# A transformer block on one core: the bias table written from 128 partitions, its other traffic on a second queue, and the experts' gathers issued one pair ahead

## The reference

```python
x = x + attn(layernorm(x))              # 16 heads, additive bias by distance, causal, then a small MLP
x = x + xattn(layernorm(x), ctx, ctx)   # 8 heads, differential weights, then an MLP with two norms
x = x + ffn(layernorm(x))               # 8 experts, each token goes to the nearest centroid's expert

# in attn
bias = rel_bias[bucket]                          # (S, S, 16), bucket depends on key - query alone
attn = (einsum(q, k) + bias) * scale             # scale: one factor per head
attn = softmax(where(causal, attn, -1e6))
# in ffn, for the expert e of a token
h = xn @ up_w[e]; a, g = split(h)
out = (a * silu(g)) @ down_w[e] + skip
```

## Time and profile before

| | us |
|---|---|
| three runs: lowest, median, highest | 1495.56, 1496.47, 1498.79 |
| the profiled execution, whole | 1503.02 |
| its span, on which all rows lie | 1501.3 |
| first score product of stage A starts | 73.56 |
| first expert product starts | 1205.11 |

### The profile page before, as it was taken

One profiled execution on the slowest core, in us unless ns is written; L12 is line 12 of the kernel. 1 busy time (PEld: TensorE's weight loads), 2 busy tenths in 40 slices (PEclk: granted clock), 3 DMA queues, 4 the chain that ended last, 5 costly groups with the idle time before them and its releaser, 6 DMA issues.

```text
span 1501.3 us, 27047 instructions
## 1 busy us (share of the span) xinstructions
PE 1287.7 (86%) x8806; PEld 933.9 (62%) x8807; DVE 813.5 (54%) x2080; ACT 554.3 (37%) x1179; POOL 429.2 (29%) x657
## 2 busy tenths in 40 slices
PE   3187999999999999999999999999997288888887
PEld 1055767777676777767677776767775145555544
DVE  3245566765768667576767757686654611211111
ACT  1224353543535354363635445363531022121211
POOL 2110203231322324132232413223222333434342
PEclk9578999999999999999999999999999589999998
DMA  6910000000000000000000000000063011111111
GB/s 90 288 31 15 1 15 11 20 28 0 28 0 28 4 24 23 5 28 0 28 0 28 18 10 28 0 28 8 16 230 134 14 50 51 53 49 49 48 59 25
DMA packets 44483, 58.77 MB, mean 39 GB/s; under 512 B 6549, under 2 KB 38111, under 8 KB 44192
## 3 DMA queue, kind: packets, MB, share of 16 engines
q1 hardware_dynamic: 38832, 43.87, 10.1%
q0 software_dynamic: 5616, 14.43, 3.3%
HBM read 42.54 MB, written 16.66 MB: 39 GB/s over the span
## 4 chain that ended last, share of the span: by engine, by line
PE 54%; DVE 16%; issue 11%; POOL 7%; ACT 5%; DMA 5%; SPq 3%; POOLq 0%; DVEq 0%; ACTq 0%
PE bank L1302 49%; DMA shared<-rows_x,shared 4%; POOL shared L883 3%; ACT shared L700 2%; PE bank L1464 2%; DVE a_p L1121 2%; POOL out_rows L901 2%; ACT a_p L695 1%; DVE a_sq L1081 1%; SPq L552 1%; DVE shared L998 1%; PE bank L1323 1%; POOL shared L778 1%; DVE shared L953 1%; DVE shared L1090 1%
## 5 line engine op out<-in xcount | busy, mean ns | idle before, releaser
L1302 PE MATMUL bank<-shared 128*128 128x256 f32 (+4 forms) x2242 | 449.9, 381 | 35.3 <-POOL shared L878 11.3
L1302 PEld LDWEIGHTS bank<-shared 128*128 128x128 f32 (+2 forms) x2242 | 319.4, 174 | 115.9 <-issue 32.4
L1121 DVE TENSOR_TENSOR a_p<-a_p,eb 128x385 f32<-128x385 f32 x256 | 125.9, 555 | 75.7 <-ACT a_p L695 75.7
L1302 PE MATMUL bank<-up,shared 128*128 x312 | 139.6, 601 | 0.9 <-issue 0.9
L845 POOL TENSOR_SCALAR a_rz<-a_ms 128x2 f32<-128x2 f32 x16 | 3.1, 193 | 418.8 <-ACT a_sq L706 418.8
L695 ACT ACTIVATE a_p<-bank 128x385 f32<-128x385 f32 x256 | 105.2, 503 | 41.6 <-PE bank L1302 41.5
L1302 PE MATMUL bank<-a_xnT,w 128*128 128x256 f32 x512 | 114.7, 382 | 1.4 <-ACT a_xnT L612 1.4
L1302 PE MATMUL bank<-w,a_hT 128*128 128x256 f32 x512 | 113.1, 379 | 0.0
L1302 PEld LDWEIGHTS bank<-a_xnT,w 128*128 128x128 f32 x512 | 96.0, 190 | 18.0 <-issue 3.4
L1302 PEld LDWEIGHTS bank<-w,a_hT 128*128 128x128 f32 x512 | 97.3, 190 | 13.2
L961 DVE TENSOR_SCALAR shared<-shared 128x256 f32<-128x256 f32 x128 | 67.5, 578 | 68.3 <-POOL shared L778 62.2
(11 more groups left out here) (197 smaller groups left out, 2128.9 us busy)
## 6 DMA issues: line engine op xcount, KB each, us to landing
up<-in_L_ffn_up_w SPq DMA_DIRECT2D x8, 1024.0 KB, 13.8
x_in<-in_x SPq DMA_DIRECT2D x16, 256.0 KB, 2.7
shared<-in_ctx SPq DMA_DIRECT2D x16, 256.0 KB, 2.9
rows_x<-shared SPq DMA_DIRECT2D x16, 256.0 KB, 2.2
rows_skip<-shared SPq DMA_DIRECT2D x16, 256.0 KB, 2.3
down<-in_L_ffn_down_w SPq DMA_DIRECT2D x8, 512.0 KB, 12.3
toep<-a_hT SPq DMA_DIRECT2D x1, 3072.0 KB, 33.3
eb<-toep SPq DMA_DIRECT2D x2, 1024.0 KB, 7.4
```

What stands on the lines that cost most here:

```text
L1121: tt(a_p[:, n_ % NPA], a_p[:, n_ % NPA], eb[:, n_], ALU.mult).then_inc(sig["a_p"], 1)
L1302: return mm(out, lhsT=lhsT, rhs=rhs, start=first, stop=last, **kw)
```

## The change

**The bias.** The scale is multiplied into the 32 x 16 table ahead of the product, and the table is laid eight times side by side (`COPIES = 8`), so that the product gives every head's row on eight partitions, 128 in all. `toep` is written from these 128 partitions, each of which writes 16 of the 128 copies of its head. The loads that this needs go first on SP. The value and output weights, the write of the maxima and their read back are issued by ACT, on its own DMA queue, at the head of its program. Subtraction, exponential and mask work on four parts of four heads, and each group of scores waits for its own part. `w0v` is scaled ahead of the first turn, and the first batch's `A.v` stands where that of the other batches does.

**The experts.** `m_in` of pair k + 2 is gathered in step k, once the tiles of pair k + 1 have been transposed, and the gathers of pairs 0 and 1 are issued ahead of the first step. PE's order within a pair is new: the second tile's up product is split around the first tile's transpose, and the next pair's `transpose_in` stands ahead of the second tile's down product.

```diff
-    mrow = nc.dram_tensor("mrow", (H0, S), F32, kind="Internal")
+    mrow = nc.dram_tensor("mrow", (H0, COPIES, S), F32, kind="Internal")
...
-    bd = flat_h[0:H0, S:S + 3 * P]
-    bmax = flat_h[0:H0, S + 3 * P:2 * S + 3 * P]
+    bd = flat_h[:, S:S + 3 * P]
+    bmax = flat_h[:, S + 3 * P:2 * S + 3 * P]
+    relb_rows = flat_h[0:BUCKETS, 2 * S + 3 * P:2 * S + 4 * P].rearrange("b (h g) -> b h g", g=COPIES)
...
     def _(sp):
+        for dst, src in bias_loads:
+            sp.dma_start(dst, src).then_inc(s_bias, 16)
         sp.dma_start(x_in[:], of_batch(x_tiles, 0)).then_inc(sig["a_loaded"], 16)
...
         sp.wait_ge(s_bd, 2)
-        sp.dma_start(toep.ap(), bd.unsqueeze(1).to_broadcast([H0, P, 3 * P])).then_inc(s_toep, 16)
-        sp.wait_ge(s_bmax, 2)
-        for t in range(T):
-            sp.dma_start(mrow.ap()[:, tok(t)], bmax[:, tok(T - 1 - t)]).then_inc(s_toep, 16)
-        for dst, src in v_loads:
-            sp.dma_start(dst, src).then_inc(s_v, 16)
-        sp.wait_ge(s_toep, 48)
+        by_row = toep.ap().rearrange("h (g i) m -> (h g) i m", g=COPIES)
+        sp.dma_start(by_row, bd.unsqueeze(1).to_broadcast([P, P // COPIES, 3 * P])).then_inc(s_toep, 16)
+        sp.wait_ge(s_toep, 16)
...
     def _(act):
+        for dst, src in v_loads:
+            nc.scalar.dma_start(dst, src).then_inc(s_v, 16)
+        act.wait_ge(s_bmax, 2)
+        by_row = mrow.ap().rearrange("h g q -> (h g) q")
+        for t in range(T):
+            nc.scalar.dma_start(by_row[:, tok(t)], bmax[:, tok(T - 1 - t)]).then_inc(s_mrow, 16)
         act.wait_ge(s_setup_dma, ALL_LOADED)
         nc.scalar.activation(lam[:, 1:2], lam[:, 0:1], ACT.Exp, scale=-1.0).then_inc(s_lam, 1)
+        act.wait_ge(s_mrow, 16 * T)
+        maxima = mrow.ap()[:, 0].rearrange("(o h) q -> o h q", o=1)
+        for half, loaded in enumerate((s_tp1, s_tp2)):
+            nc.scalar.dma_start(bias_max[half], maxima[:, half * 8:(half + 1) * 8, :].to_broadcast([P, 8, S])
+                                ).then_inc(loaded, 16)
...
-        def step(k, n, nxt):
+        def step(k, n, nxt, nxt2):
             for u in range(n):
                 after_tile(act, "m_up", k, u)
                 nc.scalar.activation(m_sg[:, u], bank[3 + 2 * u][:], ACT.Silu).then_inc(mig[u]["m_silu"], 1)
+                after_tile(act, "m_ht", k, u)
+                copy(m_hT[:, u].rearrange("p j s -> p (j s)"), bank[H_BANK[u]][:]).then_inc(mig[u]["m_hT"], 1)
             for u in range(nxt):
                 transposed(k + 1, u)
-            for u in range(n):
-                after_tile(act, "m_ht", k, u)
-                copy(m_hT[:, u].rearrange("p j s -> p (j s)"), bank[H_BANK[u]][:]).then_inc(mig[u]["m_hT"], 1)
...
+        for u in range(2):
+            after_tile(pool, "m_x", 0, u)
+            gather(m_in, rows_x, sorted_row[:, 2 + u:3 + u], "m_loaded", u)
+
+        def step(k, n, nxt, nxt2):
+            for u in range(nxt2):
+                after_tile(pool, "m_x", k + 1, u)
                 after_tile(pool, "m_row", k, u)
                 gather(m_in, rows_x, m_row[:, 0, u], "m_loaded", u)
...
-        dve.wait_ge(s_setup_dma, ALL_LOADED)
+        dve.wait_ge(s_bias, BIAS_LOADED)
+        tt(relb_rows, bc(relb[:], COPIES), bc(qscale[0:BUCKETS, 0, 0:H0], COPIES), ALU.mult).then_inc(s_relb, 1)
         dve.wait_ge(s_bd, 1)
         dve.wait_ge(s_pe_setup, 1)
-        ts(bd[:, P:P + S], bank[0][0:H0, 0:S], sc16[:, 0:1], None, ALU.mult).then_inc(s_bd, 1)
+        dve.tensor_copy(bd[:, P:P + S], bank[0][:, 0:S]).then_inc(s_bd, 1)
...
+            after_tile(pe, "m_xT", k, 0)
+            after_tile(pe, "m_h", k, 0, 0)
+            after_tile(pe, "m_hT", k, 1, 0)
+            up_half(0, 0)
+            up_half(0, 1).then_inc(mig[0]["m_up"], 1)
+            if n == 2:
+                after_tile(pe, "m_xT", k, 1)
+                after_tile(pe, "m_h", k, 1, 0)
+                after_tile(pe, "m_out", k, 1, 0)
+                up_half(1, 1)
+            turn_hidden(0)
+            if n == 2:
+                up_half(1, 0).then_inc(mig[1]["m_up"], 1)
+            down_tile(0)
+            if n == 2:
+                turn_hidden(1)
+            for u in range(nxt):
+                transpose_in(k + 1, u)
+            if n == 2:
+                down_tile(1)
```

More of the change, by code:

```diff
@@ L419, in _build @@
     ]
-    setup_loads += [(qscale[:, t, 0:H0], on_all(d["L0_attn_scale"])) for t in range(T)]
     qk_loads = [(w0qk[:, :, 0:D], w_view(d["L0_attn_Wq"])), (w0qk[:, :, D:], w_view(d["L0_attn_Wk"]))]
@@ L556, in _ @@
             sp.dma_start(eb[:, :, tok(t)], shifted).then_inc(s_tp, 16)
-        maxima = mrow.ap().rearrange("(o h) q -> o h q", o=1)
-        for half, loaded in enumerate((s_tp, s_tp2)):
-            sp.dma_start(bias_max[half], maxima[:, half * 8:(half + 1) * 8, :].to_broadcast([P, 8, S])
-                         ).then_inc(loaded, 16)
         for dst, src in a_loads:
@@ L891, in _ @@
             gather(m_skip, rows_skip, sorted_row[:, u:u + 1], "m_skip", u)
-        def step(k, n, nxt):
-            for u in range(nxt):
-                after_tile(pool, "m_x", k, u)
+        for u in range(2):
[4 more added lines that the diff above has]
+                after_tile(pool, "m_x", k + 1, u)
                 after_tile(pool, "m_row", k, u)
@@ L939, in subtract_maxima @@
         def subtract_maxima():
-            for half in range(2):
-                dve.wait_ge(s_tp, 48)
-                if half == 1:
-                    dve.wait_ge(s_tp2, 16)
-                heads = slice(8 * half, 8 * half + 8)
-                tt(eb[:, heads, S:S + P], eb[:, heads, P:S], bias_max[half][:, :, 0:P], ALU.subtract).then_inc(s_eb, 1)
-                dve.wait_ge(s_eb, 2 * half + 1)
-                tt(eb[:, heads, 0:S], eb[:, heads, 0:S], bias_max[half], ALU.subtract).then_inc(s_eb, 1)
+            dve.wait_ge(s_tp, 16 * T)
+            for q in range(H0 // GROUP):
+                if q % 2 == 0:
+                    dve.wait_ge((s_tp1, s_tp2)[q // 2], 16)
+                heads = slice(GROUP * q, GROUP * q + GROUP)
+                top = bias_max[q // 2][:, GROUP * (q % 2):GROUP * (q % 2) + GROUP]
+                tt(eb[:, heads, S:S + P], eb[:, heads, P:S], top[:, :, 0:P], ALU.subtract).then_inc(s_eb, 1)
+                dve.wait_ge(s_eb, 2 * q + 1)
+                tt(eb[:, heads, 0:S], eb[:, heads, 0:S], top, ALU.subtract).then_inc(s_eb, 1)
         def stats(x, st, mv, s_stats, s_mv, batch):
@@ L1103, in turn @@
                 subtract_maxima()
-                scale_rows(w0v, 0, s_v, V_LOADED)
             if Cc:
@@ L1119, in turn @@
                 for n_ in n if (what, st) == ("score", "A") else ():
+                    if it.first == 1 and n_ % GROUP == 0:
+                        dve.wait_ge(s_masked, 3 * (n_ // GROUP) + 3)
                     taken(dve, it, f"A.s{n_}")
@@ L1207, in _ @@
             ts(w0qk[:, c], w0qk[:, c], ln0[:, 0, c:c + 1], None, ALU.mult).then_inc(s_w, 1)
+        scale_rows(w0v, 0, s_v, V_LOADED)
         dve.wait_ge(s_const, CONSTS)
@@ L1274, in of_tile, with step @@
             return r_id[:, which, i:i + 1] if isinstance(i, int) else r_id[:, which, bass.ds(i, 1)]
-        def step(k, n, nxt):
-            for u in range(nxt):
-                after_tile(dve, "m_loaded", k, u)
-                ts(m_row[:, 0, u], of_tile(3, 2 * k + 2 + u), 1.0, None, ALU.mult).then_inc(mig[u]["m_row"], 1)
+        def step(k, n, nxt, nxt2):
             for u in range(n):
@@ L1282, in step @@
                 tt(m_h[:, u], bank[2 + 2 * u][:], m_sg[:, u], ALU.mult).then_inc(mig[u]["m_h"], 1)
+            for u in range(nxt2):
+                after_tile(dve, "m_loaded", k + 1, u)
+                ts(m_row[:, 0, u], of_tile(3, 2 * k + 4 + u), 1.0, None, ALU.mult).then_inc(mig[u]["m_row"], 1)
             for u in range(n):
@@ L1424, in turn @@
                 transposes(it, "B.x", b_xl)
-            if A and it.first > 1:
+            if A:
+                if it.first == 1:
+                    pe.wait_ge(s_v, V_LOADED)
+                    pe.wait_ge(s_w, 2 * C)
                 rows_out(it, "A.v", a_xnT, w0v)
@@ L1469, in turn @@
                 cols_out(it, "D.h3", b_zT, w11, 6)
-            if it.first == 1:
-                pe.wait_ge(s_v, V_LOADED)
-                pe.wait_ge(s_w, 2 * C)
-                rows_out(it, "A.v", a_xnT, w0v)
             if Bb:
@@ L1622, in step, with down_tile @@
                 ins.then_inc(mig[u]["m_ht"], 1)
-            for u in range(n):
+            def down_tile(u):
                 after_tile(pe, "m_hT", k, u)
```

75 lines of the change are left out of this document (35 added, 40 removed).

## The result

The changed kernel takes 1466.02 us, the median of 4 runs (1461.77 to 1467.62), against 1497.63 for the kernel before beside it. The ratio is 0.9774, with an interval of 0.9752 to 0.9796: faster by 31.6 us, less than half of what was forecast, and above the range. On the profiled executions the span falls from 1501.3 to 1465.9 us, by 35.4.

What follows compares the result with a forecast made beforehand. TensorE was taken to bound the kernel, with removable waits at the start and in the expert pairs: -26 and -47 us make -73, a span of 1428. Forecast 1425, own range 1412 to 1438; with rivals 1 to 3, 1410 to 1446.

Steps and rivals of the forecast that it cites:

- rival 1: Start: the bias table's write stays slow, limited by the DRAM side or its 2048 pieces; 17 us lost, 1442; 12%.
- rival 2: Start: ACT is held by its DMA queue, its copy moves to about 27 us; 8 us lost, 1433; 15%.
- At 300 GB/s the 7.3 MB from 9.5 on take 24 us and end at 34: Start: bias table write, maxima read beside it and eb behind it share 300 GB/s, so subtraction starts at 34, not 57.30.
- The prediction's own test, first scores after 55: Start: the prediction counts as wrong if first scores start after 55 us; it expected them at 46 to 49.
- The chain behind the first subtraction: Start: subtraction, meeting POOL's masks, last exponential, ACT's work and handing over take 13.3 us, giving scores at 47.3.
- Its own sign of being wrong, pairs above 13 us: Experts: the prediction counts as wrong if pairs keep above 13 us; it expected 12.0 to 12.6.
- From one pair to the next I take 0.1 us, what separates the last down slot from the next up in the quick pair: Experts: TensorE's gap between one pair's last down product and the next pair's first up product is 0.1 us.
- The pair's terms: Experts: 11.6 us without a wait, 0.6 for ACT's copy and 0.1 between pairs give 12.3 a pair, 221.4 for 18.
- rival 3: Experts: pairs get only part, by a wait counted as covered, a held up tile or longer slot; 13.3 us, 1443; 13%.

Runs made afterwards that it cites:

- the run on SP: Changed kernel with the two reads of the maxima issued by SP behind eb's, not by ACT; eight copies and 8 KB pitch stay: 1456.30 us (0.9716).
- With one block: Changed kernel with one copy of the maxima, so each half is read as one block of 8 KB: 1447.06 us (0.9633) with this edit alone.
- Written out: Changed kernel with the loop over the expert pairs written out, no branch, same instructions: 1454.83 us (0.9677).
- both losses mended: Changed kernel with one copy of the maxima, its reads on SP behind eb's, and the expert pairs written out: 1435.46 us (0.9564).
- The control with a pitch of 8 KB: Changed kernel with only the first copy of the maxima written, its rows still 8 KB apart, reads on ACT's queue: 1460.43 us, one run.

## Why the prediction went wrong

**The start: right in the write, wrong in the read behind it.** `toep` is issued at 8.51 (predicted 8.3) and lands in 11.3 us (10); the rate on 128 partitions is as the row of the store had it, and rival 1 falls. ACT's copy is at 19.48 (18 to 21), so rival 2 falls. The step that failed is "At 300 GB/s the 7.3 MB from 9.5 on take 24 us and end at 34". It took the read of the maxima at the rate of the kernel before, though the diff gives the tensor a dimension more: its rows move from 1 KB to 8 KB apart. The read ran at about 80 GB/s (by itself, in the run on SP) and pulled `eb` down with it, to the first subtraction at 52.91 instead of 34. With one block it is at 33.93 to 35.6, as predicted. The prediction's own test, first scores after 55, caught it at 66.68. None of the rivals named it. The chain behind the first subtraction, put at 13.3 us, is 15.0 with four parts (13.8 in the changed kernel, whose late start spares it GpSimd's other work).

**The experts: right in the waits and the clock, wrong at the pair's end.** No wait for gathered rows is left, the clock is 1.00, and the wait for ACT's copy is 0.33 us (0.6 predicted). Its own sign of being wrong, pairs above 13 us, came true with 13.12. The step that failed is "From one pair to the next I take 0.1 us, what separates the last down slot from the next up in the quick pair". In that quick pair sixteen down products stood behind the last wait and hid the branch; the new order leaves eight. The pair's terms were 11.6 of work, 0.6 for ACT and 0.1 between pairs. They measure 12.16 (by the rows of 1257.69 to 1270.81: up 6.97 where 6.9 was put, down 3.71 for 3.5, transposes 1.48 for 1.2), 0.33 and 0.63: 13.12 instead of 12.3. The work was put too low by nearly as much as the pause, 0.56 against 0.53, but part of that is the tail of the last down products, which the next up covers when nothing pauses: written out, a pair takes 12.4. Over 18 pairs it is 12.9 us: 234.3 against 221.4. Written out, they take 223.7. The size is that of rival 3 (13.3 us), but its mechanism, a wait for VectorE, does not show. The prediction also argued as if the gathers and the new order each removed a part. Each removes the whole wait for gathered rows, and the order has a price of its own in a loop.

**The sum.** The forecast span was 1428, the measured one is 1465.9: 37.9 us more, of them 19.4 at the start, 13.8 from the experts on and 4.7 between. With both losses mended the span is 1434.0: 3.4 more than forecast at the start (first scores at 50.66), 3.2 from the experts on, and 0.6 less between. The part between the marks was forecast as unchanged. It took 1131.6 us before, 1136.3 after, and 1128.1 to 1136.5 in the kernels of the study, whose code is the same there. The rows show where it goes: the same 32 products take 7.17 us before and 10.04 after. In the 10 us that lie 20 to 30 us behind the first scores the granted clock is 0.99 before and 0.58 after (before first, then after):

```profile
95.43 7.17 PE L1302 MATMUL bank<-a_xnT,w 128*128 128x256 f32 x32 [0.68 <-ACT a_xnT L612]
93.56:103.56 10.00, 8.79 (x42) 7.60 (x43) 2.09 (x7) 3.78 (x9) 4.62 (x10) 0.99 0.01 2
```

```profile
89.15 10.04 PE L1317 MATMUL bank<-a_xnT,w 128*128 128x256 f32 x32 [0.68 <-ACT a_xnT L622]
86.68:96.68 10.00, 8.65 (x26) 6.88 (x27) 2.23 (x7) 2.58 (x7) 4.62 (x10) 0.58 0.00 1
```

That is 2.9 of the 4.7 us. All 18 traces divide in this way: where the clock from 30 to 60 us behind the first scores has a mean of 0.94, the part takes 1128.1 to 1131.8 us, and where it has 0.87 to 0.89, 1132.1 to 1136.5. The control with a pitch of 8 KB starts its scores as late as the changed kernel and yet takes 1129.2, so late scores do not bring it about. What does, no run here shows, and each trace is one execution. Between two medians some microseconds can be this and not the edit.

**The baseline.** The forecast was set against a median of 1496.47, 6.55 below the profiled execution. Beside the later sets the same kernel had 1499.37 to 1501.85. So 3 to 5 us of the distance between 1425 and the 1435.46 of the mended kernel are this.

## What to carry to other kernels

When an edit adds a dimension to a tensor in DRAM, look at the distance between the rows that a transfer reads, and not at its bytes alone; keep the rows together, or pad them off a power of two, as 9 KB and 1152 bytes did here. A slow transfer does not only come late: it slows the ones beside it on another queue, so the wait shows on another tensor. Before an order of work in a loop is changed, count what the engine has queued between its last wait and the branch, and if two edits remove the same wait, try each by itself.

## What the runs showed of the hardware that was not expected

- A read of eight 1 KB rows by all 128 partitions (1 MB) lands in 7.3 to 9.7 us with rows 1 KB, 1152 bytes or 9 KB apart, in 14.3 to 15.1 with 4 or 12 KB, and in 23.8 to 24.5 with 8 KB.
- The DMA engines count as 84% busy at 69 GB/s while this goes on (20 to 25 us in the changed kernel), and as 99% at 82 GB/s when the slow read runs by itself (35 to 40 us in the run on SP). The write of the bias table before had a share of 0.88 at 100 GB/s. A high DMA share is no sign that a transfer is near the engines' rate.
- A loop's branch with eight short products (1.99 us) behind TensorE's last wait leaves a pause of 0.63 us; with sixteen (3.54 us) there is none.
- The same code can get TensorE's clock of 2.4 GHz later in one execution than in another. 20 to 30 us behind the first scores, which come at 66.68 and 65.98, the changed kernel was granted 0.58 and the control 0.98; between the marks they take 1136.3 and 1129.2 us.
